# The last stage of a recurrence and the routing of a mixture, joined in one plan

## The reference

```python
        o_flat = ((o - mu) * jax.lax.rsqrt(var + EPS)).reshape(Bn, Tn, C) * gn_weight + gn_bias
        bonus = ((rh * kh * r_k).sum(-1, keepdims=True) * vh).reshape(Bn, Tn, C)
        o_flat = o_flat + bonus
        return o_flat * g @ W_o
...
        tokens = _layer_norm(tokens, ln_gamma, ln_beta)
        logits = tokens.astype(jnp.float32) @ gate_weight.astype(jnp.float32).T
        probs = jax.nn.softmax(logits, axis=-1)
        top1 = jnp.argmax(logits, axis=-1)
        onehot = jax.nn.one_hot(top1, E, dtype=jnp.int32)
        rank_e = jnp.cumsum(onehot, axis=0) - onehot
        rank = jnp.sum(rank_e * onehot, axis=-1)
        keep = rank < CAPACITY
        dispatch = dispatch.at[top1, slot].add(tokens * keep[:, None])
        h = jax.nn.gelu(jnp.einsum('ech,ehi->eci', dispatch, wi), approximate=False)
        expert_out = jnp.einsum('eci,eih->ech', h, wo)
        out = (residual + combined).reshape(inputs.shape)
...
    x = x + _L0_attn_b_ref(_layernorm(x, axis=-1), ...)
    x = x + _L0_ffn_ref(_layernorm(x, axis=-1), ...)
```

## Time and profile before

| | us |
|---|---|
| median of 3 runs | 4496.63 (4488.98 to 4498.77) |
| the profiled execution, own time | 4498.68 |
| its span, from first to last instruction | 4497.0 |
| `finish` and second routing, of that span | 3936 to 4243 |
| the eight experts of the second mixture | 4243 to 4497 |

### The profile page before, as it was taken

How to read it: one execution, slowest core, us unless ns; L and a number is a source line. 1 busy time by engine, 2 the same in 40 slices (tenths; PEclk the granted TensorE clock), 3 DMA queues, 4 the chain that set the end, 5 groups by cost and what they waited for, 6 DMA issues and landing times. The chain is left out here.

```text
span 4497.0 us, 72210 instructions
## 1 busy us (share of the span) xinstructions
PE 3958.5 (88%) x23448; PEld 2701.7 (60%) x23448; DVE 3213.0 (71%) x8691; ACT 2185.5 (49%) x7329; POOL 2053.9 (46%) x1670
## 2 busy tenths in 40 slices
PE   5999999999996696888849999999999999846698
PEld 2344444444435464666538888888888888745566
DVE  5777777877746111889869999999999999855310
ACT  2666666666665111544404555556555555503311
POOL 2211221221223321112258888888888888632522
PEclk7999999999996798999979999999999999976699
DMA  4322332332347132244353232323232222186332
GB/s 110 82 75 70 99 80 67 91 83 65 75 96 224 63 130 80 103 168 168 149 101 39 34 42 34 42 34 42 35 41 36 39 37 38 14 283 209 130 126 80
DMA packets 495672, 395.16 MB, mean 88 GB/s; under 512 B 298634, under 2 KB 457637, under 8 KB 489184
## 3 DMA queue, kind: packets, MB, share of 16 engines
q1 hardware_dynamic: 483040, 365.68, 33.0%
q0 software_dynamic: 12288, 25.28, 1.7%
HBM read 230.52 MB, written 167.97 MB: 89 GB/s over the span
## 5 line engine op out<-in xcount | busy, mean ns | idle before, releaser
L749 DVE TENSOR_REDUCE at_neg_max<-at_slot 128x1 f32<-128x512 f32 (+3 forms) x1216 | 746.1, 655 | 247.5 <-PE at_slot L541 244.7
L671 ACT ACTIVATE at_prob<-at_slot 128x512 f32<-128x512 f32 (+1 forms) x1216 | 631.1, 577 | 354.8 <-PE at_slot L561 353.8
L1722 PE MATMUL sc_added<-sc_outer,sc_ident 128*128 128x128 f32 x4096 | 585.9, 286 | 79.3 <-POOL sc_outer L1473 58.2
L1722 PEld LDWEIGHTS sc_added<-sc_outer,sc_ident 128*128 128x128 f32 x4096 | 496.4, 191 | 210.1 <-DVE sc_state L1623 115.4
L1486 POOL TENSOR_TENSOR sc_terms<-sc_seen,sc_pack 128x1024 f32<-128x1024 f32 (+2 forms) x288 | 605.6, 2150 | 13.7 <-PE sc_ps_o L1744 13.7
L1744 PE MATMUL sc_ps_o<-sc_terms,sc_ident 128*128 128x256 f32 x2048 | 607.0, 381 | 2.1 <-POOL sc_terms L1486 2.1
L389 POOL TENSOR_SCALAR_AFFINE_SELECT at_prob<-at_prob 128x512 f32<-128x512 f32 x256 | 162.8, 636 | 888.3 <-ACT at_prob L671 888.1
L1646 ACT ACTIVATE sc_seen<-sc_state 128x512 f32<-128x512 f32 x256 | 152.8, 597 | 757.1 <-DVE sc_decayed L1587 748.1
L541 PE MATMUL at_slot<-at_k_stack,at_q_stack 96*128 96x512 bf16 (+3 forms) x1536 | 459.4, 335 | 22.2 <-DMA at_k_stack<-parts 19.8
L1473 POOL TENSOR_TENSOR sc_outer<-sc_pack 128x2048 f32<-128x2048 f32 x128 | 467.3, 3671 | 5.0
L561 PE MATMUL at_slot<-at_q_stack,at_k_stack 99*128 99x512 bf16 (+3 forms) x1536 | 452.7, 331 | 12.2 <-ACT at_prob L671 11.8
(11 more groups left out here) (251 smaller groups left out, 7164.1 us busy)
## 6 DMA issues: line engine op xcount, KB each, us to landing
packed<-pr_pack SPq DMA_DIRECT2D x16, 3072.0 KB, 13.4
sc_pack<-packed SPq DMA_DIRECT2D x512, 96.0 KB, 3.6
parts<-at_parts SPq DMA_DIRECT2D x96, 256.0 KB
f_up_w<-in_ffn_wi SPq DMA_DIRECT2D x16, 1024.0 KB
f_down_w<-in_ffn_wo SPq DMA_DIRECT2D x16, 1024.0 KB
at_q_stack<-parts SPq DMA_DIRECT2D x32, 384.0 KB
at_k_stack<-parts SPq DMA_DIRECT2D x32, 384.0 KB
slots<-at_no_row SPq DMA_DIRECT2D x2, 4128.0 KB
```

The source lines that it names most:

```text
L671: act.activation(prob[:, first:first + n, q1 - tiles * P:q1], ps[:, 0:n * tiles * P].rearrange("p (n k) -> p n k", n=n), ACT.Exp)\
L749: dve.tensor_reduce(neg_max[:, chunk, qt, h:h + n], ps[:, 0:n * tiles * P].rearrange("p (n k) -> p n k", n=n), AX.X, ALU.max, negate=True) ...
L1722: pe.matmul(added[h][:, 0:HALF], ident[:], outer[m % 2][:, 2 * n + s, h * HALF:(h + 1) * HALF], start=(s == 0), stop=False)
```

## The change

`finish` is gone, and so is the DRAM tensor x_recurred. The routing of a mixture is now one of two functions: `route_alone`, which is the old code and serves the first mixture, and `finish_and_route`, which serves the second and does the work of `finish` too. It has one list of jobs, `finish_plan`, that all engines walk through in the same order, each doing its own part of a job; no hardware loops. The sum with the residual stays in the x buffer and the statistics, token rows and base rows read it there. PSUM has six slots of 128x512 f32 in one ring, so transposes, products and their copies are half or a quarter of a batch each. `wait_read` makes an engine wait until a job's slot was emptied.

```diff
...
+FINISH_SLOTS = 6
+FINISH_USER = {"y_turn": "act", "y_out": "dve", "r_turn": "act"}
+
+
+def finish_plan():
+
+    def of(stage, b):
+        return [(stage, b)] if 0 <= b < BATCH else []
+
+    def parts(stage, b):
+        if not 0 <= b < BATCH:
+            return []
+        if stage == "y_out":
+            return quarters(stage, b)
+        return [(stage, (b, c, half)) for half in range(2) for c in range(KC)]
+
+    plan = of("bias", 0) + of("weigh_o", 0)
+    for b in range(BATCH + 2):
+        plan += of("weigh", b - 2) + of("bias", b + 1) + parts("y_turn", b) + parts("r_turn", b - 1) + of("count", b - 2)
+        plan += parts("y_out", b) + of("gate", b - 1) + of("stats", b) + of("place", b - 2)
+        plan += of("weigh_o", b + 1) + of("affine", b) + of("choose", b - 1)
+    return plan
...
+            def load_outputs(b):
+                k = b % 2
+                for dst, src in ((o, feed.o_in), (bonus, feed.bonus_in), (og, feed.gate_in)):
+                    sp.dma_start(dst[k][:], rows(src, b)).then_inc(in_ready[k], 16)
...
+            load_outputs(0)
+            sp.dma_start(w[:], feed.w_o.rearrange("(k p) n -> p k n", p=P)).then_inc(out_in, 16)
+            load_x(0)
...
+            load_outputs(1)
+            load_x(1)
+            load_x(2)
+            for b in range(BATCH):
+                if b + 2 < BATCH:
+                    slots.wait_read(sp, *y_turns(b), alone=True)
+                    load_outputs(b + 2)
+                sp.wait_ge(base_ready, 1 + b + 1)
+                sp.nop(nofuse=True)
+                sp.dma_start(rows(x_out, b), base[b % 2][:]).then_inc(base_stored[b % 2], 16)
+                if b + XBUFS < BATCH:
+                    sp.wait_ge(tok_ready, 1 + b + 1)
...
+                if stage == "bias":
+                    b = what
+                    if b == 0:
+                        pool.wait_ge(norm_in, 1 + 32)
+                    pool.wait_ge(in_ready[b % 2], 1 + 48 * (b // 2 + 1))
+                    pool.tensor_tensor(bonus[b % 2][:], bonus[b % 2][:], bias_wide, ALU.add).then_inc(with_bias, 1)
+                elif stage == "place":
...
+            for stage, what, s, use in plan.jobs:
+                if s is not None:
+                    ps = slot[s]
+                    slots.wait_empty(pe, s, use)
+                if stage == "y_turn":
+                    b, c, half = what
+                    if (c, half) == (0, 0):
+                        pe.wait_ge(gated, 1 + b + 1)
+                    for n in range(HALF_TILES):
+                        last = pe.transpose(ps[:, n * P:(n + 1) * P],
+                                            o[b % 2][:, half * HALF_TILES + n, c * P:(c + 1) * P], ident[:])
+                elif stage == "y_out":
+                    b, quarter = what
+                    if (b, quarter) == (0, 0):
+                        pe.wait_ge(out_in, 1 + 16)
+                    if quarter in (0, 2):
+                        slots.wait_read(pe, *[("y_turn", (b, c, quarter // 2)) for c in range(KC)])
+                    for n in range(2):
+                        t = 2 * quarter + n
+                        for c in range(KC):
+                            last = pe.matmul(ps[:, n * C:(n + 1) * C], y_turned[:, c, t * P:(t + 1) * P], w[:, c, :],
+                                             start=(c == 0), stop=(c == KC - 1))
+                elif stage == "r_turn":
+                    b, c, half = what
+                    if (c, half) == (0, 0):
+                        pe.wait_ge(tok_ready, 1 + b + 1)
+                    for n in range(HALF_TILES):
+                        last = pe.transpose(ps[:, n * P:(n + 1) * P],
+                                            tok[b % TBUFS][:, half * HALF_TILES + n, c * P:(c + 1) * P], ident[:])
+                elif stage == "gate":
...
+            for stage, what, s, use in plan.jobs:
+                if stage == "weigh":
+                    b = what
                     act.wait_ge(shifted, 1 + b + 1)
                     if b >= 2:
                         act.wait_ge(weighed, 1 + b - 1)
                     act.activation(exps[b % 2][:], work[:], ACT.Exp).then_inc(exp_ready, 1)
-
-                for b in range(BATCH):
+                elif stage in ("y_turn", "r_turn"):
+                    b, c, half = what
+                    slots.wait_filled(act, s, use)
+                    if b and (c, half) == (0, 0):
+                        if stage == "y_turn":
+                            slots.wait_read(act, *[("y_out", (b - 1, q)) for q in range(4)])
+                        else:
+                            act.wait_ge(gate_ready, 1 + b)
+                    dst = y_turned if stage == "y_turn" else turned
+                    act.activation(dst[:, c, half * BANK:(half + 1) * BANK], slot[s][:], ACT.Copy)\
+                       .then_inc(emptied[s], 1)
+                elif stage == "stats":
+                    act.wait_ge(var_ready, 1 + what + 1)
+                    act.activation(std[:], roots[:], ACT.Sqrt).then_inc(std_ready, 1)
+                elif stage == "affine":
...
+            def weigh_o(b):
+                k = b % 2
+                dve.wait_ge(in_ready[k], 1 + 48 * (b // 2 + 1))
+                own.link(dve.tensor_tensor(o[k][:], o[k][:], weight_wide, ALU.mult))
+                dve.wait_ge(with_bias, 1 + b + 1)
+                own.link(dve.tensor_tensor(o[k][:], o[k][:], bonus[k][:], ALU.add))
+                dve.tensor_tensor(o[k][:], o[k][:], og[k][:], ALU.mult).then_inc(gated, 1)
+
+            def add_x(b, quarter, s, use):
+                slots.wait_filled(dve, s, use)
...
+            def statistics(b):
+                slots.wait_read(dve, *[("y_out", (b, q)) for q in range(4)])
...
+                elif stage == "y_out":
+                    add_x(*what, s, use)
+                elif stage == "stats":
+                    statistics(what)
+                elif stage == "place":
+                    weight_of(what)
+                    route(what)
+                elif stage == "affine":
+                    normalise(what)
+                elif stage == "choose":
+                    choose(what)
...
-    finish(nc, x_mixed, o, gate, bonus, rw["gn_weight"], rw["gn_bias"], rw["W_o"], x_recurred)
-    mixture(nc, 1, x_recurred, *experts, slots[1], tiles(out))
+    mixture(nc, 1, x_mixed, *experts, slots[1], tiles(out),
+            Feed(o, gate, bonus, rw["gn_weight"], rw["gn_bias"], rw["W_o"]))
...
```

More of the change, by code:

```diff
@@ L1 @@
+from collections import namedtuple
 from contextlib import ExitStack, contextmanager
@@ L782, in mixture @@
+def mixture(nc, n, x_in, gate_w, gamma, beta, w_in, w_out, slots_dram, x_out, feed=None):
     with ExitStack() as outer:
@@ L1110, in mixture @@
+        shared = Shared(ident, gamma_c, beta_c, gate_w, gamma, beta, slots_dram, x_out, consts, load_weights)
+        if feed is not None:
+            finish_and_route(nc, x_in, feed, shared, sb, psum, sem)
+        else:
+            route_alone(nc, x_in, shared, sb, psum, sem)
         with ExitStack() as ctx:
@@ L2349, in tiles @@
         return ap.rearrange("b (n p) c -> (b n) p c", p=P)
-    x_attended, x_mixed, x_recurred = (dram(n, (NT, P, C)) for n in ("x_attended", "x_mixed", "x_recurred"))
+    x_attended, x_mixed = (dram(n, (NT, P, C)) for n in ("x_attended", "x_mixed"))
     slots = [dram(f"slots{n}", (KEPT, ROW)) for n in range(2)]
```

985 lines of the change are left out of this document (565 added, 420 removed).

## The result

The changed kernel took 4470.56 us (median of 5 runs, 4465.41 to 4476.45), the kernel before 4495.85 (5 runs, 4488.98 to 4498.77): ratio 0.9948, 95% interval [0.9934, 0.9963], 0.5% faster. Three later comparisons gave 0.9966, 0.9977 and 0.9967. The forecast was 4497 us, no change, in a range of 4475 to 4520. The profiled execution took 4475.04 us, span 4473.3.

The account below looks back on a forecast made before the run. No engine is full; one batch's serial loop bounds both stages. The removed 21.5 us gap is used up by collisions, blocks and a 30.2 us loop against 28.8: -0.2 us, giving 4496.4, stated as 4497, range 4475 to 4520.

Parts of the forecast that it names:

- The instant that it counted to: VectorE's start on batch 7's token rows: 4201.4 against 4201.63 before; the 41.3 us from there to the experts taken alike.
- The seven intervals: Merged loop, token rows of one batch to the next: 27.0 us, then 30.2, four of 31.0, last 23.3.
- the block: GpSimd's bonus sum holds up VectorE's onehot in choose, so the product starts later: 3.2 us over four intervals.
- step 2: TensorE's transposes and count matmuls after the token rows: the output product may start at 8.7 us.
- step 3: GpSimd's place ends at 3.8 us and its bonus sum starts, delaying onehot to 8.6 and the sums to 9.5.
- step 4: TensorE's output product, 32 matmuls: 8.5 us, chosen nearer the cold row (9.02) than the warm time (7.17).
- the collision: GpSimd's bonus sum meets VectorE's weigh_o: 4.4 us, once before batch 0's token rows, once in interval 0 to 1.
- First and fifth step: ScalarE's first copy 5.64 us after token rows starts, done at 6.2; VectorE from product to next token rows, 13.0 us.
- The fill: Start of the merged stage: batch 0's gated at 3963.5, its first token rows at 3992.5, including 4.4 us for bonus-sum interference.
- The tail: From batch 7's token rows to the experts: last choices, two batches of indirect writes, a barrier; 41.3 us, unchanged.
- Transfers costed at nothing: A loop's 6.3 MB at 261 GB/s would alone hold it at 24 us, below 31, so no cost.
- The faster rival: 4475 to 4489 us, chance 0.31: bonus sums outside weigh_o (-8.8), none in choose (-3.2), warm product in seven intervals (-9.1).

## Why the forecast was wrong

The instant that it counted to was the right one: all of the difference between the forecast's row load (4242.7) and the measured 4219.40 comes from its terms. The seven intervals, forecast 208.9 us and measured 189.6, hold 19.3 of the 23.3 us. Term by term, summed over the seven:

| term of the sum | forecast | measured | less |
|---|---|---|---|
| token rows to product, without the block (step 2) | 58.9 | 51.7 | 7.2 |
| the block (step 3) | 3.2 | 0 | 3.2 |
| the product (step 4) | 59.5 | 51.0 | 8.5 |
| VectorE behind the product, with the collision | 87.3 | 86.9 | 0.4 |

- **Third step, the mechanism that failed: "it ends at 11.1 - 7.3 = 3.8, and the bonus sum of b+2 starts there".** The sum starts at 6.96, since three writes beside weigh_o take 2.0 to 2.1 us and not 1.0; onehot is through by then, and no block comes. In the sum it is only 3.2 us, but put back it makes up for the other terms too: the product then starts at 9.7 (forecast 9.5), takes 8.4 to 9.9 (forecast 8.5), and the kernel takes as long as before. The forecast weighed this with "SBUF — State Buffer" of the Trainium skill, section on who interferes with whom, and set it aside for want of a row: what that section says of a VectorE instruction with two SBUF inputs and a GpSimd one that reads SBUF fits the writes (2.0 to 2.1 us beside weigh_o, 0.98 without), though VectorE's operations keep their 2.29 us. Its inference that such an operation leaves descriptor generation alone does not fit these writes. The 3.2 us worked out there counted the block alone.
- **Second step, "the product may start at 8.7": 7.5.** The third and fourth token block took 1.15 us and not 1.84, and the count 0.24, not 0.6. TensorE's clock had already risen (1.00 from 4079.30 to 4080.50).
- **Fourth step, the product at 8.5: 7.07 to 7.15** in six of eight batches, 8.2 in the other two. This was the largest mis-sized term. The choice went to the cold row because TensorE idles ahead of its transposes; it idles 9.3 us and the product is warm in most loops all the same. With the 16 token transposes moved behind it, it takes 8.7 to 10.0. "TensorE: Matmul & The Clock Gate" of the Trainium skill, part 1, says that idleness brings the low state back: the trace agrees for the 24 transposes behind those 9.3 us (0.50). That the product behind them would be cold as well did not come true: the clock had risen within the transposes.
- **First and fifth step right**: first copy 5.66 for 5.64; 12.96 us from product end to token rows for 13.0.
- **The fill**: gated(0) at 3959.37, 4.1 us earlier than the 3963.5 taken over; 2.8 of it is the barrier ahead of the stage, by code that didn't change. From there to the first token rows 27.7 us for 29.0. Both collisions came, 6.47 us for 2.29, as forecast.
- **The tail**: 42.7 us for 41.3; 40.3 to 42.7 in four profiles of the changed kernel. VectorE's wait ahead of L1477 there is 5.8 us in the profile with 42.7 and 4.3 in the two with 41.2.
- **Transfers costed at nothing**: right, and more slack than thought.

The faster rival named two of its three causes rightly (no block, warm product); its third, sums outside weigh_o, did not happen. Its 0.31 was too little chiefly because one unseen fact, the held write, took the block away and, by the run with the block, with it a cold product in four loops. That the first comparison came out below even this rival's range is in part scatter: it has the largest of four gains.

Left open: why four comparisons give gains of 25, 15, 9 and 15 us, when the changed stage is the same within 2.2 us. The old stages vary (8 us between two profiles), and so do the unchanged ones ahead (8.9 us on one chip); which of the two made the 9 was not profiled.

## What to carry to other kernels

Before pricing a small GpSimd or VectorE operation by its length, ask which instruction of the other engine it lands beside: here 2.6 us in the start of one sum moved the whole kernel by 18 us. The merge took out a gap of 21.5 us and a quarter of the traffic; the traffic was worth nothing, and the merged loop (27.6 us) is hardly shorter than the two loops together (28.8). The order of the plan is worth more: moving the wait-free work (the next batch's gating) into another engine's wait, with separate PSUM rings and the other repairs, gave 49 us more without one instruction less.

## What the hardware showed beyond the forecast

- An indirect write takes 0.98 us on GpSimd alone and 2.0 to 2.1 beside VectorE's 2.29 us two-input operations. In the loop shown the operation ends at 4095.64 (4093.36 + 2.28), the write that began during it at 4096.52 (4094.39 + 2.13), 0.88 us behind: nearly a whole write. The one that began 0.03 us behind such an operation took 3.11. Single-input operations of 1.34 us hold it too (1.8 us), those of the token rows (256 elements each) don't (0.98).
- A VectorE operation of 8 elements (`f_earlier`) waits out a whole GpSimd sum, 4.74 us, though by the trace it began 0.18 us ahead of the sum (4076.32, 4076.50).
- The same product took 7.15 us at a granted clock of 1.00 and 8.79 where the clock began at 0.55. The fall came just ahead of the product, behind pauses of TensorE of 1.1 to 2.2 us. Pauses of 1.2 to 1.8 us stand ahead of warm products too, so their length alone doesn't decide it.
- VectorE's waits for TensorE's results, with no instruction that ended just before the release, came to 36.0 us in one routing of before and to 5.8 in the merged stage; the cause is open.
